# Gating of the expert tiles moved to the head of each place of VectorE's and ScalarE's order, in the third phase of a four-layer kernel

## The reference, cut to what matters

```
x = x + L2_xattn(layernorm(x), ctx)     # 16 heads of 8
x = x + L2_ffn(layernorm(x))            # slot router: top 8 of 64, softmax, a GRU step, mix
x = x + L3_xattn(layernorm(x), ctx)     # 16 heads of 64
x = x + L3_ffn(layernorm(x))

def L3_ffn(x):                          # 8 experts, top 2
    shared = (silu(x @ sw1) * (x @ sw2)) @ sw3
    probs  = softmax(x @ rw + rb);  w, idx = top_k(probs, 2);  w = w / sum(w)
    gates  = scatter(w at idx)
    h      = silu(x @ ew1[e]) * (x @ ew2[e])
    return shared + sum over e of gates[e] * (h @ ew3[e])
```

## Time and profile before

| | before |
|---|---|
| median of three runs | 2343.54 us |
| the profiled execution | 2347.68 us |
| its span, first to last instruction | 2345.9 us |
| mean granted TensorE clock | 0.907 of full |
| TensorE matmuls busy | 1911.0 us (81%) |
| VectorE busy | 1507.8 us (64%) |
| ScalarE busy | 1292.4 us (55%) |
| GpSimd busy | 630.4 us (27%) |

### The profile page before, as it was taken

How to read it: one execution, slowest core, us unless ns; L and a number is a source line. 1 busy time by engine, 2 the same in 40 slices (tenths; PEclk the granted TensorE clock), 3 DMA queues, 4 the chain that set the end, 5 groups by cost and what they waited for, 6 DMA issues and landing times.

```text
span 2345.9 us, 49910 instructions
## 1 busy us (share of the span) xinstructions
PE 1911.0 (81%) x17542; PEld 1551.2 (66%) x17544; DVE 1507.8 (64%) x3920; ACT 1292.4 (55%) x4431; POOL 630.4 (27%) x626
## 2 busy tenths in 40 slices
PE   3987998888899984477888889888989888888774
PEld 2776877777787772256566667777767766666663
DVE  5987776777778985555655755656556464645342
ACT  2765655556566664355676656565556544544421
POOL 0003031422211300132333332442433413232421
PEclk9988999999999996577899998997989999999987
DMA  7002444443543002100000112211212222222253
GB/s 221 29 15 94 123 142 141 127 137 118 153 136 104 29 6 106 54 18 10 23 1 19 37 29 76 77 58 59 74 53 72 67 71 77 76 76 82 86 155 109
DMA packets 125126, 184.21 MB, mean 79 GB/s; under 512 B 10320, under 2 KB 82064, under 8 KB 124624
## 3 DMA queue, kind: packets, MB, share of 16 engines
q1 hardware_dynamic: 116688, 164.23, 23.0%
q0 software_dynamic: 8192, 16.79, 2.3%
HBM read 145.52 MB, written 35.45 MB: 77 GB/s over the span
## 4 chain that ended last, share of the span: by engine, by line
PE 35%; DVE 10%; ACT 6%; issue 6%; POOL 1%; DMA 1%; SPq 0%; DVEq 0%; ACTq 0%; POOLq 0%
PE ps L1614 6%; PE ps L1863 4%; ACT pb L2003 4%; PE ps L1842 3%; PE ps L1849 3%; PE ps L1652 3%; PE ps L1636 2%; PE ps L1643 2%; DVE nm L2355 2%; PE ps L1625 2%; PE ps L1821 2%; PE ps L1670 1%; DVE hT L2146 1%; ACT pt L2011 1%; DVE hT L2141 1%
## 5 line engine op out<-in xcount | busy, mean ns | idle before, releaser
L2003 ACT ACTIVATE pb<-ps,nm 128x128 f32<-128x128 f32 x1024 | 363.3, 377 | 264.2 <-DVE nm L2355 264.0
L2044 POOL TENSOR_TENSOR pb<-pb,rcs 128x512 f32<-128x512 f32 x256 | 266.7, 1042 | 803.3 <-DVE rcs L2344 802.3
L968 ACT ACTIVATE pb<-pb,nm 128x128 f32<-128x128 f32 x1024 | 313.0, 392 | 81.7 <-DVE nm L1191 81.7
L2355 DVE TENSOR_REDUCE nm<-ps 128x8 f32<-128x1024 f32 x128 | 156.0, 1219 | 139.3 <-PE ps L1849 72.1
L2364 DVE COPY pt<-ps 128x512 f32<-128x512 f32 x128 | 88.3, 690 | 220.0 <-PE ps L1863 220.0
L2003 ACT ACTIVATION_READ_ACCUMULATOR pb<-ps,nm 128x1 f32 x1024 | 222.0, 217 | 0.0
L1863 PE MATMUL ps<-w,pb 128*128 128x128 f32 x1024 | 174.2, 297 | 49.2 <-ACT pt L2011 42.9
L1614 PE MATMUL ps<-hT,big 128*128 128x128 f32 x960 | 151.4, 308 | 58.7 <-DVE hT L2146 42.6
L1614 PEld LDWEIGHTS ps<-hT,big 128*128 128x128 f32 x960 | 134.9, 216 | 83.8 <-DVE hT L2146 58.1
L1863 PEld LDWEIGHTS ps<-w,pb 128*128 128x128 f32 x1024 | 128.3, 153 | 79.8 <-issue 66.6
L1191 DVE TENSOR_REDUCE nm<-pb 128x8 f32<-128x1024 f32 x128 | 156.1, 1220 | 4.4
(11 more groups left out here) (367 smaller groups left out, 4419.7 us busy)
## 6 DMA issues: line engine op xcount, KB each, us to landing
big<-in_we SPq DMA_DIRECT2D x92, 514.0 KB, 3.6
big<-in_we SPq DMA_DIRECT2D x120, 384.0 KB, 3.1
big<-sorted_in SPq DMA_DIRECT2D x8, 960.0 KB, 6.1
sorted_out<-big SPq DMA_DIRECT2D x28, 256.0 KB
sorted_in<-big SPq DMA_DIRECT2D x4, 1472.0 KB, 12.1
sorted_out<-h_all SPq DMA_DIRECT2D x16, 256.0 KB
hidden<-h_all SPq DMA_DIRECT2D x7, 512.0 KB, 2.9
h_all<-hidden SPq DMA_DIRECT2D x7, 512.0 KB, 3.7
```

The lines of the kernel that those rows point to most:

```text
L968: m = a.activation(pb[:, n % 2, k * S:(k + 1) * S], pb[:, n % 2, k * S:(k + 1) * S], ACT.Exp, bias=nm[:, n % 2, k:k + 1])
L2003: m = a.activation(pb[:, n % 2, e * S:(e + 1) * S], ps[:, score_bank(n) + half, k * S:(k + 1) * S], ACT.Exp, bias=nm[:, n % 2, e:e + 1], a ...
L2044: g_.tensor_tensor(p4, p4, r4.unsqueeze(2).to_broadcast([P, 4, S]), ALU.mult).then_inc(n2["p_normed"], 1)
L2355: v.tensor_reduce(nm[:, n % 2, :], ps[:, bank:bank + 2, :].rearrange("p a (j k) -> p (a j) k", k=S), AX, ALU.max, negate=True).then_inc(n2 ...
```

## The change

VectorE's loop over `hidden_rows` moves from the end of `work` to its start, for both places. ScalarE's loop over `evacuations` moves to the start for place 1, and stays at the end for place 2. Nothing else is changed: the same instructions run on the same engines with the same waits, and TensorE's, GpSimd's and the DMA queue's order stay as they were.

```diff
@@ ScalarE
                 def work(place, hs):
+                    if place == 1:
+                        for item in evacuations(place, hs):
+                            tile(*item)
                     g = slot_at(hs, 2)
...
                         router_act(a, gates[:, 0:G, :], g + 1)
-                    for item in evacuations(place, hs):
-                        tile(*item)
+                    if place == 2:
+                        for item in evacuations(place, hs):
+                            tile(*item)
@@ VectorE
                 def work(place, hs):
+                    for item in hidden_rows(place, hs):
+                        tile(*item)
                     chunk = QK_AT.get(hs)
...
                         combine(g)
-                    for item in hidden_rows(place, hs):
-                        tile(*item)
-
```

## The result

| | before | after |
|---|---|---|
| median (4 runs each, same chip) | 2340.68 us (2331.56 to 2347.81) | 2269.74 us (2262.41 to 2271.47) |
| the profiled execution | 2347.68 us | 2271.47 us |
| its span | 2345.9 us | 2269.7 us |
| mean granted TensorE clock | 0.907 | 0.919 |
| TensorE matmuls busy | 1911.0 us | 1882.4 us |

The ratio after to before is 0.9693 (95% interval 0.9651 to 0.9735). The forecast was 2298 us, with a range from 2266 to 2334; the first rival, the clock that recovers as well, said 2270.

The account below looks back on a forecast made before the run. TensorE bounds the expert-tile stretch, idling for VectorE's late gating. 60.3 us of waits less 22.8 of costs is 37.5; with 9 of clock, 46 us less: 2298 us median, range 2266 to 2334 (forecast's own 2280 to 2314).

Parts of the forecast that it names:

- the first rival: TensorE's clock recovers as well: 37.5 + 37 = 74 us less, 2270 us; sign: third-phase clock 0.98; chance 0.21.
- The gating waits: TensorE's waits before hidden matmuls and turns for VectorE's gating, expert-tile stretch: 60.3 us go, from 78 to some 20.
- The costs of the order: Work pushed back on VectorE and later copies on ScalarE give back 22.8 us, leaving 37.5 us net.
- Masked queries: VectorE's L2200 comes 0.83 us later in nine places where TensorE's scores wait for it: 7.5 us lost.
- Slot states: VectorE's L2297, which TensorE waits for twice, comes later: 2 x 0.83 = 1.7 us lost.
- The copy of the expert rows: L1901, needed by the router's matmul, is delayed by the slot router in two late groups: 3 us given back.
- The copy of V: On ScalarE, unmoved, it holds the Q matmul in two places, so 2 x 1.3 = 2.6 us given back.
- ScalarE's half: Silu ahead of the copy of Q at place 1 wins nothing and costs 8 us, bounds nothing to 23.
- The clock: Slow TensorE matmuls behind gating waits: bounds 18 us lost, 37 gained; 9 gained taken as the middle.
- The rival "time given back": TensorE meets attention's own chain at the next wait, so short gains vanish: 2330 us; chance 0.18.
- The rival "slower": TensorE waits next for what is pushed back; at 65 such places 2360 us; chance 0.06.
- The tail: After the last attention unit, waiting for weights from DRAM (14.7 us in six waits): keeps its length.

Follow-up runs that it names:

- e1: The changed kernel with ScalarE's loop put back to the end of `work`, so only VectorE's half of the change; 2266.29 us, ratio 0.9689 to before.
- e2: The changed kernel with VectorE's loop put back to the end of `work`, so only ScalarE's half of the change; 2345.03 us, ratio 1.0034 to before.
- e5: The changed kernel with VectorE's combine put back ahead of the gating, nothing else; 2285.72 us, ratio 0.9772 to before.
- e8: The kernel before with 20 unread 128 x 128 matmuls put into TensorE's two 3.68 us waits behind the combine; 2334.4 us, ratio 0.9983.
- e3: The kernel before with VectorE's gating moved ahead of the combine but behind everything else; 2326.01 us, ratio 0.9947.
- e10: The kernel before with only VectorE's masked queries moved from place 2 to the head of place 1; 2311.18 us, ratio 0.9864.

## Why the prediction was right, and where it was off

**The gating waits: right.** 60.3 us of 77.9 were to go, leaving 17.6; 62.2 went and 15.7 are left. The pieces before the hidden matmuls are at most 0.7 us; before the turns one of 1.6 us remains. The order of the gating behind L2367 or L2358 is as told. The mean clock of the stretch is 0.98, the sign that I had given for the first rival.

**The costs of the order: near in sum, off in the parts.** Predicted 22.8 us; the whole idle time fell by 43 to 44 and not 37.5, so some 18 to 19 were given back; the waits named below make 17.0 of them. That the first part (7.5 us) came out at 7.7 is luck, as its pieces show.
- Masked queries: L1842's wait was to grow from 11.2 to about 19; it is 18.9. The 7.7 us are not nine times 0.83, though. Three waits grew by 0.85 (0.32 to 1.17), as costed. Three grew by 0.34 to 0.37 (2.7 to 3.04): there L2200 (L2206 after) took 0.86 us and no longer 1.28. Three grew by 1.38 (0.72 to 2.10), since the loop over `hidden_rows` carries one more instruction that I had not counted, the addition of the shared experts' result to x (L2138, after L2142), which went ahead of the masked queries too. VectorE at the first of them:

```profile
1389.95 0.69 DVE L2367 COPY pt<-ps 128x512 f32<-128x512 f32 x1 [2.66 <-PE ps L1863]
1390.56 0.68 DVE L2142 TENSOR_TENSOR x_all<-ps,x_all 128x512 f32<-128x512 f32 x1
1391.15 0.41 DVE L2145 SCALAR_TENSOR_TENSOR hT<-hT,ps 128x256 f32<-128x256 f32 x1
1391.60 0.42 DVE L2150 SCALAR_TENSOR_TENSOR hT<-ps,hT 128x256 f32<-128x256 f32 x1
1391.94 0.86 DVE L2206 TENSOR_SCALAR qm<-qT,w 128x128 f32<-128x128 f32 x4
```

- Slot states: 0.7 paid (3.7 to 4.4), 1.7 predicted. The copy of the expert rows: a new wait of 1.9, 3 predicted. The copy of V: 15.0 to 18.6 before L1636, 3.6 paid, 2.6 predicted.
- ScalarE's half: 8 predicted, 3.1 us of new wait before L1643. In time it gains nothing, as told: e1 equals after, and e2 is 5 us slower than before. But that its early silus win nothing was wrong: with VectorE's half they shorten the gating waits by 4 us (e1 against after), so its net cost is about nothing and not 8.

**The clock: the term that was off.** It read "Bounds: 18 lost, 37 gained. I take 9 gained, the middle of the two." Measured, the slow loss between 1360 us and the tail fell from 47.0 to 11.9, and the busy time of TensorE by 31.7 us: a gain of 32 to 35 in this pair of executions. By the medians it is some 26, an estimate: 70.9 less the 43.7 of idle time and the 0.8 of the tail. Either is far above 9. The stretch shrank by 29 us more than forecast (75.4 against 46.5), and 23 of these are clock, 6 idle time. The middle was no estimate, only a place between two ends. The rows could have told more. Of the slow loss in the stretch, some 15 us lay behind the two waits of 3.68 us, and both were to shrink to under 1 us. Against them stood three waits that were to grow by at most 0.83. e5 (the combine's waits put back, slow groups behind them) and e8 (the wait filled with matmuls, clock 0.57 to 0.91 and 0.83) show that the long wait brings the slow stretch. The lower bound hardly came: behind the three waits of 3.04 us after loses 10.2 us, where before lost 5.2 (2.0, 1.3 and 1.9) behind the same three. That is 5 us more, not 18.

The Trainium skill (TensorE: Matmul & The Clock Gate, "What's actually happening") says that slow is the default and activity releases the clock. I had written that by this rule nearly all of the 37 us would come back, and that the trace agreed only in part. Most of it came back; e8, where useless activity in place of idle time was enough, agrees with the rule. What I held against it, that similar waits did and did not bring a slow stretch, still holds. e1 has the order of after on VectorE and TensorE. The matmuls behind its first wait of 3.03 us ran at full clock, and those behind its second, of 3.04, did not:

```profile
1455.75 1.16 PE L1842 MATMUL ps<-xm,qm 32*128 32x128 f32 x16 [3.03 <-issue]
...
1595.49 2.08 PE L1842 MATMUL ps<-kT,qm 32*128 32x128 f32 x16 [3.04 <-issue]
```

In after all three such waits had slow matmuls behind them. I can't say what decides it.

**Where the time fell.** 2269.74 us lies outside the range of the forecast itself (2280 to 2314) and inside the wide one only as the case of the first rival, which I had given 0.21. Its mechanism came. That its 2270 us was met so closely is partly luck: in the profiled pair the idle time fell by 6 us more than in its sum (37.5 + 37) and the clock gave 5 less.

**The rival "time given back": real, but not here.** In e3, with only the combine's waits cut, the idle time came back elsewhere (119.5 to 118.4), part of it where faster matmuls met the next gating wait, and in e10 the idle time hardly fell either (119.5 to 116.6). It did fall in the whole change, since all the waits of the step shrank together. That is how I read the three; no run splits the change finely enough to show it.

**The rival "slower": did not happen.** Eleven pushed-back places were certain by my count. The waits of the list above that are new or longer are 22 (nine of L1842, two of L1749, two of L351, three more of L1636, six of L1643), not the 65 that it needed.

**The tail: right.** 123.1 against 123.9 us, with the weights as its wait. Before the hidden matmuls, answering to the earlier trace rows:

```profile
PE ps L1614 <- DMA big<-in_we: 12.8, 6, 2.7
```

## What to carry to other kernels

On an in-order engine that serves two chains, put first what releases the buffer that the bounding engine writes next, and count the price at the work that moves behind it: here one wait grew from 11 to 19 us, and moving what it waits for ahead as well gave another 45 us, 26 of them ahead of the tiles. Price a wait of TensorE not by its length alone: where the rows show slow matmuls behind it, as behind those of 2.7 to 3.7 us here, add that time, and look for them a few groups further on too. Expect most of it back when the wait goes, less what the next wait takes: in e3 and e8 1.4 us at each place. Cutting one wait of a step alone can bring nothing but the clock (e3), since the next one in line takes the time.

## What the hardware showed that I had not expected

- The 20 fp32 matmuls of e8 are 40 records, and took 4.73 us, 0.24 us for each matmul.
- Moving four small VectorE instructions of the masked queries (0.86 us together) by one place was worth 30 us alone and 45 us after the change, more than the combine (14) or the gating at place 1 (19) by itself.
- The two gating instructions, which read PSUM, took 0.39 to 0.43 us each in before and after, beside GpSimd or not. The four instructions of the masked queries, which read and write SBUF, took 0.86 to 0.88 us together with GpSimd idle. In three steps of before with tiles the first of them started beside GpSimd's division (L2044); it alone then took 0.69 us and not 0.28, and the four took 1.28.
